# Reordering the start of an attention stage and moving one scaling of the token tiles from ScalarE to GpSimd

## The reference, cut to what matters

```python
def _div_clamp_fp8(x, scale):
    y = jnp.clip(x.astype(jnp.float32) / scale, -FP8_MAX, FP8_MAX)
    y = y.astype(jnp.bfloat16).astype(jnp.float32)
    return _fp8_roundtrip(y)

ln_out = _ln(hidden_states, ln_w, ln_b)
q  = _fp8_linear_pertensor(ln_out, wq,  wq_scale,  q_in_scale)    # _div_clamp_fp8 inside
qx = _fp8_linear_pertensor(ln_out, wqx, wqx_scale, qx_in_scale)
k  = _fp8_linear_pertensor(ln_out, wk,  wk_scale,  k_in_scale)
v  = _fp8_linear_pertensor(ln_out, wv,  wv_scale,  v_in_scale)
```

## Time and profile before

| what | value |
|---|---|
| median of three executions | 1367.06 us |
| the profiled execution's own time | 1364.38 us |
| its span on the core | 1362.6 us |
| PE busy | 1261.7 us, 93% |
| DVE busy | 1091.9 us, 80% |
| ACT busy | 948.1 us, 70% |
| POOL busy | 703.0 us, 52% |

### The profile page before, as it was taken

How to read it: one execution, slowest core, us unless ns; L and a number is a source line. 1 busy time by engine, 2 the same in 40 slices (tenths; PEclk the granted TensorE clock), 3 DMA queues, 4 the chain that set the end, 5 groups by cost and what they waited for, 6 DMA issues and landing times.

```text
span 1362.6 us, 28116 instructions
## 1 busy us (share of the span) xinstructions
PE 1261.7 (93%) x10492; PEld 1089.8 (80%) x10492; DVE 1091.9 (80%) x2205; ACT 948.1 (70%) x2152; POOL 703.0 (52%) x616
## 2 busy tenths in 40 slices
PE   0588999999999999999999999879999899995998
PEld 0578899999999999999999999866776344544998
DVE  7979989999989999989999999977335578766554
ACT  5789887778887778887788887653121466673775
POOL 4667554565655566555556454431000255563675
PEclk9879999999999999999999999999999889996999
DMA  4222232222122221132221100025554153017562
GB/s 144 80 58 78 98 92 88 75 69 67 53 79 86 77 77 57 54 88 81 74 59 34 38 25 25 20 73 144 58 81 73 42 97 69 18 33 248 206 232 82
DMA packets 117382, 110.05 MB, mean 81 GB/s; under 512 B 11995, under 2 KB 101307, under 8 KB 117120
## 3 DMA queue, kind: packets, MB, share of 16 engines
q1 hardware_dynamic: 114128, 99.03, 27.1%
q0 software_dynamic: 2944, 9.19, 1.9%
q10 hardware_dynamic: 176, 0.04, 0.0%
HBM read 80.20 MB, written 28.07 MB: 79 GB/s over the span
## 4 chain that ended last, share of the span: by engine, by line
PE 78%; DVE 13%; issue 3%; ACT 3%; DMA 2%; POOL 1%; SPq 1%; POOLq 0%; DVEq 0%; ACTq 0%
PE PC L577 8%; PE SS L543 7%; PE PO L559 7%; PE B L521 5%; PE PA L479 4%; PE PA L481 4%; PE B L1201 3%; PE B L1686 3%; PE PO L1185 2%; PE PA L492 2%; PE PA L491 2%; PE PA L493 2%; PE SS L535 2%; PE SS L2186 2%; PE PA L504 2%
## 5 line engine op out<-in xcount | busy, mean ns | idle before, releaser
L1000 POOL TENSOR_TENSOR RB<-YS,M 128x512 bf16<-128x512 f32 x128 | 161.3, 1260 | 279.0 <-DVE YS L860 279.0
L665 ACT ACTIVATE QT<-B,sm 128x256 f32<-128x256 f32 x256 | 131.4, 567 | 141.8 <-PE B L521 141.3
L479 PE MATMUL PA<-WH,XQ 128*128 128x256 f32 x512 | 140.7, 306 | 23.8 <-POOL XQ L941 19.1
L995 POOL TENSOR_TENSOR yy<-vv,half 128x14 f32<-128x14 f32 (+1 forms) x64 | 147.6, 2307 | 5.3
L543 PE MATMUL SS<-QT,KT 128*128 128x256 f32 x512 | 133.1, 383 | 6.9 <-DVE mx L812 6.6
L481 PE MATMUL PA<-WL,XQ 128*128 128x256 f32 x512 | 129.9, 286 | 0.0
L824 DVE TENSOR_REDUCE vv<-SQ 128x7 f32<-128x896 f32 (+1 forms) x128 | 120.6, 942 | 0.3 <-ACT SQ L711 0.3
L479 PEld LDWEIGHTS PA<-WH,XQ 128*128 128x128 f32 x512 | 98.8, 193 | 25.0 <-issue 19.5
L832 DVE TENSOR_TENSOR QN<-QN,yy 128x512 f32<-128x512 f32 x128 | 114.3, 893 | 0.0
L812 DVE TENSOR_REDUCE mx<-SS 128x4 bf16<-128x512 f32 x128 | 87.9, 687 | 26.2 <-PE SS L535 25.3
L521 PE MATMUL B<-identf,QN 128*128 128x128 f32 x768 | 105.7, 274 | 2.0 <-ACT LNT L620 2.0
(11 more groups left out here) (344 smaller groups left out, 4117.7 us busy)
## 6 DMA issues: line engine op xcount, KB each, us to landing
W<-in_w SPq DMA_DIRECT2D x16, 1024.0 KB
XK<-xk_d SPq DMA_DIRECT2D x24, 512.0 KB, 4.3
V<-v_d SPq DMA_DIRECT2D x112, 64.0 KB
v_d<-VST SPq DMA_DIRECT2D x48, 128.0 KB, 2.0
Q<-qsc SPq DMA_DIRECT2D x48, 128.0 KB
WR<-in_wprojT SPq DMA_DIRECT2D x16, 256.0 KB, 3.0
xk_d<-XK SPq DMA_DIRECT2D x8, 512.0 KB, 3.9
kt_d<-KT SPq DMA_DIRECT2D x64, 64.0 KB, 1.7
```

Of the source, the lines that this page charges most:

```text
L479: pe.matmul(PA[:, 256 * k:256 * k + 256], XQ[:, k, c, bs], wh[:, c, 256 * k:256 * k + 256], start=c == 0, stop=False)
L665: a.activation(QT[i % 2][:, o:o + 256], B1[:, o:o + 256], ACT.Identity, bias=col(n + "b"), scale=col(n + "w"))
L995: p.tensor_tensor(yy[j % 2][:, :, 0:n], v_, half[:, 0:2 * n].rearrange("p (h k) -> p h k", h=2), ALU.pow).then_inc(s_rstd, 1)
L1000: p.tensor_tensor(RB[i % 2][:], YS[:], M[:], ALU.subtract).then_inc(s_rb, 1)
```

## The change: what it does

Four things are changed; the arithmetic of the rounded tiles stays the same.

1. **GpSimd makes QY of tiles 8 to 31.** A new function `pool_quad_scale` (L941 in the changed file) multiplies 128x512 of `LNT` by the reciprocal scale, a per-partition operand read from `scn`, and writes bf16. It is called for both tiles of a step at the head of POOL's step, ahead of `pool_rstd`. ACT makes `QY` of the first eight tiles only, and still all `QM`.
2. **Semaphores.** The new `s_qy` counts POOL's QY tiles. DVE's rounding of tile i waits for it as well as for `s_qm`; ACT waits for it before it writes the next quad into `LNT`. `s_cx`, for which nobody waited, is gone.
3. **DVE's and ACT's prologue.** DVE rounds tiles 0 to 3 at once, then does both `WL` and only then the variances of quad 1. ACT makes both `WH` after tile 3.
4. **POOL's prologue.** The first weights are centred first, and multiplied by the smoothing factors (`RSM`, `RSV`, which come through a DMA of their own) after the first and the second clamped tile. The root of quad 1 comes after tile 3.

```diff
@@ act_quad_turned
                 if q4 and c == 0:
                     a.wait_ge(s_qm, 8 * q4)
+                if q4 > 1 and c == 0:
+                    a.wait_ge(s_qy, 8 * q4 - 8)
@@ act_quad_scale
-            if i >= 3:
-                a.wait_ge(s_qs, i - 2)
-            a.activation(QY[i % 3][:], LNT[:, c], ACT.Copy, scale=scn[:, k, c:c + 1])
+            if q4 == 0:
+                if i >= 3:
+                    a.wait_ge(s_qs, i - 2)
+                a.activation(QY[i % 3][:], LNT[:, c], ACT.Copy, scale=scn[:, k, c:c + 1])
@@ act_attention_0
             for k in range(8):
                 act_quad_scale(a, 0, k)
-                if k in (1, 2):
-                    act_weights_upper(a, 0, k - 1)
                 if k == 3:
+                    act_weights_upper(a, 0, 0)
+                    act_weights_upper(a, 0, 1)
                     act_context(a, 1)
@@ dve_quad_round
             v.wait_ge(s_qm, i + 1)
+            if q4:
+                v.wait_ge(s_qy, i - 7)
@@ dve_attention_0
-            dve_variances(v, 1)
             for k in range(8):
                 dve_quad_round(v, 0, k)
-                if k in (1, 2):
-                    dve_weights_lower(v, k - 1)
+                if k == 3:
+                    dve_weights_lower(v, 0)
+                    dve_weights_lower(v, 1)
+                    dve_variances(v, 1)
                 if k == 5:
                     dve_normalised(v, 1)
@@ new on POOL
+        def pool_quad_scale(p, q4, n):
+            k, c = divmod(n, 2)
+            i = 8 * q4 + n
+            p.wait_ge(s_lnt, 2 * q4 + c + 1)
+            p.wait_ge(s_qs, i - 2)
+            p.tensor_scalar(QY[i % 3][:], LNT[:, c], scn[:, k, c:c + 1], None, ALU.mult).then_inc(s_qy, 1)
+        def pool_first_weights_centre(p, c):
+            raw = raws(0)[c]
+            p.wait_ge(s_wsc, c + 1)
+            for n_, (h, n) in enumerate(((0, 4), (5, 3))):
...
+                p.wait_ge(s_wmean, 2 * c + n_ + 1)
+                t = p.tensor_tensor(w_, w_, m.unsqueeze(2).broadcast_to([128, n, 128]), ALU.subtract)
+            t.then_inc(*ps.up())
+        def pool_first_weights_smooth(p, c):
+            raw = raws(0)[c]
+            if c == 0:
+                p.wait_ge(*ps.at())
+                p.wait_ge(s_rsm[0], 32)
+                p.wait_ge(s_rsv, 16)
+            w_ = WV0[:, c].rearrange("p (g d) -> p g d", g=2)
+            p.tensor_tensor(w_, w_, RSV[:], ALU.mult)
+            p.tensor_tensor(raw[:, 512:640], raw[:, 512:640], RSM[0][:, 0, 0], ALU.mult).then_inc(s_wcen, 1)
@@ pool_attention_0
-            pool_weights_centre(p, 0, 0)
-            pool_weights_centre(p, 0, 1)
-            pool_quad_root(p, 1)
+            pool_first_weights_centre(p, 0)
+            pool_first_weights_centre(p, 1)
             for k in range(8):
                 pool_quad_round(p, 0, k)
+                if k < 2:
+                    pool_first_weights_smooth(p, k)
                 if k == 3:
+                    pool_quad_root(p, 1)
                     pool_context(p, 1)
             pool_quad_root(p, 2)
             pool_quad_root(p, 3)
             for n in range(N + 9):
+                if quad_at(n):
+                    q4, k = quad_at(n)
+                    pool_quad_scale(p, q4, k)
+                    pool_quad_scale(p, q4, k + 1)
                 if 0 <= n - 1 < N:
                     pool_rstd(p, n - 1)
                 if quad_at(n):
-                    q4, k = quad_at(n)
                     pool_quad_round(p, q4, k)
                     pool_quad_round(p, q4, k + 1)
```

More of the change, by code:

```diff
@@ L155, in build @@
         s_x = [sem(f"x{i}") for i in range(4)]
-        s_small, s_ident, s_identb, s_th, s_cx = (sem(n) for n in ("small", "ident", "identb", "th", "cx"))
+        s_small, s_ident, s_identb, s_th, s_qy = (sem(n) for n in ("small", "ident", "identb", "th", "qy"))
         s_lguess, s_lroot = sem("lguess"), sem("lroot")
@@ L869, in dve_attention_0 @@
             v.wait_ge(s_th, 1)
-            v.tensor_tensor(cx[:], cx[:], th[:, 0:1], ALU.mult).then_inc(s_cx, 1)
+            v.tensor_tensor(cx[:], cx[:], th[:, 0:1], ALU.mult).then_inc(*vs.up())
             for k in range(4):
@@ L957, in pool_weights_scale @@
             t.then_inc(s_wsc, 1)
+        def pool_first_weights_centre(p, c):
+            raw = raws(0)[c]
+            p.wait_ge(s_wsc, c + 1)
+            for n_, (h, n) in enumerate(((0, 4), (5, 3))):
+                w_ = raw[:, 128 * h:128 * h + 128 * n].rearrange("p (h d) -> p h d", d=128)
+                m = wm[:, c, min(h, 4):min(h, 4) + n]
+                p.wait_ge(s_wmean, 2 * c + n_ + 1)
[10 more added lines that the diff above has]
+            p.tensor_tensor(raw[:, 512:640], raw[:, 512:640], RSM[0][:, 0, 0], ALU.mult).then_inc(s_wcen, 1)
         def pool_weights_centre(p, g, c):
```

## The result

The changed kernel took 1389.24 us (median of four runs, 1385.56 to 1390.95), the kernel before 1368.39 us beside it: the ratio is 1.0139 with a 95% interval from 1.0100 to 1.0179. It is slower by about 19 us, where I had forecast 2 us and a range that ended at 1379 us. The profiled execution took 1387.58 us, its span is 1385.8 us.

The account below looks back on a forecast made before the run. PE sets the end but until about 145 us waits for others, mainly DVE. The loop's start gains 3.9 us, twelve steps paced by POOL give back 5.9: a median of 1369.1 us, range 1361 to 1379.

Parts of the forecast that it names:

- the stall of step 10: Main loop: DVE could start step 10 at about 125 us but gets its tile from POOL at 129.0.
- Rival 1: Main loop: POOL keeps up and ACT's relief pays in steps 3 to 7; about 7 us faster, 1360 us; chance 0.24.
- rival 4: Whole kernel: nothing counts, small prologue gain and ACT relief cancel losses, or PE isn't ready earlier; within 3 us; chance 0.10.
- the sum of the POOL loop: Steps 0 to 11: QY, rounding, clamps, RB and tails added step by step; POOL's pace gives back 5.9 us.
- the price d of one QY: POOL's multiplication per tile in the loop: taken as 1.15 us, between 0.93 and 1.86.
- my second sign: DVE's L832 beside POOL's L956 took 0.95 instead of 0.68 us, so L956 held the shared port only about 0.27 us.
- Rival 2: QY pair heading POOL's step: factor operand paid per element, 1.6 to 1.86 us each; 10 to 13 us slower, 1379; chance 0.16.
- The prologue's gain: Before the loop: variances of quad 3 end 6.5 us earlier, at 38.8 us; the loop starts 3.9 us earlier.
- My outer bound of 3 us gain: Prologue on DVE: if no stall between rounding and WL goes, variances of quad 3 end only 3 us earlier.
- 0.35 us: Added to each loop step because POOL and DVE meet oftener on the shared port; 3.9 us in all.
- Rival 3: Main loop: the shared port is held for the whole QY, about 0.9 us a step; 8 us slower, 1375; chance 0.12.
- The ends: Whole-kernel extremes: 5.4 us faster with QY at 0.93 us and no port term, 13.4 us slower with 1.86.

Follow-up runs that it names:

- experiments 3: The changed kernel with POOL's QYs moved behind the clamps of the step before, against the kernel before: ratio 1.0121, YS of step 11 ends at 156.33 us.
- experiments 9: QYs behind the previous step's clamps, in the changed kernel, as multiplication and addition with constants (wrong values): ratio 1.0043 to the kernel before, YS of step 11 146.68 us.
- experiment 8: The changed kernel with QY as minimum and maximum against constants, same place (wrong values): ratio 1.0057 to the kernel before, YS of step 11 147.84 us.
- 1: The changed kernel's prologue alone, ACT making every QY, against the kernel before: ratio 0.9981, repeated 0.9961; YS of step 11 at 137.02 and 137.09 us.

## Why the prediction was wrong

**The place of the loss was right.** DVE and ACT full, POOL behind them in one in-order step, no gain where DVE is the bound, the stall of step 10 behind scaling and CL (forecast 127.8 + 1.15 against a DVE ready at 125; measured 143.1 against 138.6), a whole trace shifted by nearly one amount after step 11: all of this is in the rows above. Rival 1 is excluded, and so is rival 4: the shift of 17.9 us reached the end. Two signs failed: the first tile of the loop came at 45.58 us, outside 39 to 43, and POOL was busy for 87.27 of the 99 us from 41 to 140, 88% and not over 95, because in odd steps its clamps and RB wait for DVE. And that DVE waits there doesn't make the order of POOL's step the cause: moved elsewhere, the QYs gained only 4.0 and 1.2 us (experiments 3 and 9).

**The step that failed is the sum of the POOL loop: three of its terms were too small, and the price d of one QY first of all.** I read L956 as mostly fixed, because the clamp handles 512 elements in 0.61 us. But the clamp has two operations in one instruction, and L956 and QY have one. QY measured 1.56 us and not 1.15. The forms show two laws: one operation costs 0.61, 0.93 and 1.56 us on 128, 256 and 512 elements with a factor operand, thus (1.56 - 0.93) / 256 = 2.5 ns for each element; two constants cost 0.41 and 0.62 us on 256 and 512, 0.8 ns for each. My comparison mixed them. The short hold of the port beside L956, my second sign, was real (DVE's L785 takes 1.12 instead of 0.68 us beside the second QY, 0.44 us of a QY of 1.56), but says nothing on the duration. Rival 2 had the size, and not the reason: with a constant QY takes 1.49 us. By the chain of experiment 8 (12 QYs), 0.41 us more per QY are 4.9 us; by my own count of 16 they are 6.6, and step by step in my formulas, which have 17, 7.0.

**The prologue's gain was mis-sized.** Forecast: variances of quad 3 done at 38.8 us; measured 42.83, 4.0 us later. Rounding began at 17.42 us and not at 16.8, and DVE took 25.4 us from there on, not 22. I had taken out the stalls between rounding and WL, but POOL's centring, clamps and smoothing now run beside DVE's first four roundings, which took 8.0 us (to 25.45) where the pace of the loop gives 5.3, and both WL took 1.6 us each (1.63 and 1.22 before). The root of quad 3 took 1.01 us and not 1.39, so the first QY started 3.7 us late. My outer bound of 3 us gain, "if no stall goes", was nearer (2.5 us).

**The odd steps cost more than 0.35 us beside d; the even ones, but for one, did not.** With d = 1.56 and its 0.35 us my formula meets the even steps 2, 4, 6 and 10 within 0.1 us. Only step 8 is longer, 128.05 - 118.13 = 9.92 us against 9.4: a pair of QYs took 3.55 instead of 3.13 us, and two clamps 1.63 instead of 1.2. Steps 0, 3, 5, 7 and 9 are 0.6 to 1.1 us longer than the formula (step 9, from 128.05 to 141.56, 13.5 us against 12.9), and from the QYs of step 11 to the end of YS it took 1.0 us more. In these DVE's first rounding lies in the chain, and 0.44 us of the excess are its 1.12 instead of 0.68 us. From the miss of 15.9 us (144.4 to 160.34), 3.7 are the start, 4.9 to 7.0 are d, and 5.3 to 7.3 remain for such terms over twelve steps. Rival 3, the port, was thus a part of it, though not as the SBUF page of the Trainium skill has it (SBUF — State Buffer, "Who interferes with whom", the pair is held for the whole instruction): by that rule DVE's first rounding, which starts 0.1 us behind the second QY, would wait for nearly all of its 1.56 us, and it waits 0.44. Experiments 3 and 9, with QY beside DVE's rounding, show more of it.

**The ends were too near.** d = 1.86 alone gave 13.4 us; real were d = 1.56, a start 3.7 us later and a larger term per step together. I varied one unknown at a time, and all three went the same way. Two of them, the start and the term per step, have a common source as I read the rows: more work on POOL beside DVE's two-input instructions. The price d has a source of its own, the form of the instruction, and that it went the same way is chance.

## What to carry to other kernels

An engine with idle time isn't free: ask where in its order the gap lies, and what stands between its tail and the engine that waits. Another place in that order gained only 4.0 of the 17.9 us here, though. Price a new instruction only by rows of the same form; number of operations and kind of operands counted here as much as the width. And before work is moved to an engine that shares a port with the bound, try the half of the change that doesn't move work: here that half alone, measured twice, gives 0.9981 (0.9941 to 1.0022) and 0.9961 (0.9930 to 0.9992), and the whole 1.0139.

## What the runs showed of the hardware that I hadn't expected

- GpSimd's TENSOR_SCALAR from f32 to bf16 on 128x512 takes 1.49 us with one operation and a constant, 0.62 us with two operations and two constants, 1.56 us with one factor operand and 0.77 us with two. Adding a second operation with an operand of the same kind halves the time; factor operand and constant together took 1.99 us. The Trainium skill (GPSIMD Engine Reference, "Engine selection") says that one-input work is roughly line-rate on GpSimd; here the two-operation forms with operands of one kind fit that (0.8 ns an element), and one operation costs 2.5 ns an element.
- A TENSOR_TENSOR with its second input broadcast from one column takes 1.04 us, against 1.26 us with two full inputs, and less than the one-operation multiplication by the same column. The kernel before had a hint of it: its subtraction of the broadcast means on 128x512 (L974) took 1.04 us on the mean of 15.
- Instructions added on GpSimd lengthen VectorE's instructions with two inputs even where VectorE hardly waits for their results: with 24 of 0.62 us DVE was busy for 96.25 us in the stretch, and for 86.88 without them (experiments 9 and 1).
